# Routed experts in groups of 128 slots with resident down weights, in place of groups of 256 with streamed ones

## The chip, the cores and the metric

The kernel runs on one core of one Trainium2 chip. The metric is the device time of one execution in microseconds (us). A time here is a median over runs; a profile is one further execution, whose own time stands beside its span.

## The reference, cut to what matters

The program is a chain of eight layers over 32 x 128 tokens of 128 features: linear, quantised feed-forward, three attentions, three further feed-forwards. The change lies in the fourth, a mixture of 8 experts in which each token picks 2:

```python
gate_scores = jnp.einsum('bsd,ed->bse', pn, sn) / temperature
top_v, top_i = jax.lax.top_k(gate_scores, 2)
gate_probs = jax.nn.softmax(top_v, axis=-1)
comb = jnp.sum(jax.nn.one_hot(top_i, E, dtype=x.dtype) * gate_probs[..., None], axis=-2)
h = jax.nn.gelu(jnp.einsum('bsd,edf->ebsf', x, W1) + b1[:, None, None, :], approximate=False)
eo = jnp.einsum('ebsf,efd->ebsd', h, W2) + b2[:, None, None, :]
out = jnp.einsum('ebsd,bse->bsd', eo, comb)
```

Here W1 is 128 x 512 and W2 is 512 x 128 per expert, all in f32. The 4096 tokens with 2 choices each make 8192 rows to compute.

## The kernel before, in words

Each layer is one or more blocks; a block ends with all five engines at a barrier. Four blocks make the fourth layer's first part. `route_scores` (L1125) normalises the tokens and makes the scores. `top_two` (L1284) picks two experts per token. `slot_lists` (L1873) sorts the 8192 choices into groups of G x 128 slots, each group of one expert; it writes the token of each slot (`slots`), the expert of each group (`expert_of`) and the slot of each choice (`dest`). Since each expert fills whole groups, the number of groups is fixed at its worst case, NG = (8192 + 8 x (G x 128 - 1)) // (G x 128); with G = 2 that is 39 groups, 9984 slots. All groups are computed, also those that hold only spare rows. The next layer's `combine_project` (L2199) gathers two result rows per token.

`chosen_experts` (L2037) computes the groups. Per group g:

- SP (`load`, L2082) reads the expert number into a register with a value load (L2084), issues the up weights (`wu`, 256 KB, L2088) and the down weights with both biases (`wd`, 322 KB, L2091), then stores the finished group g - 3 (L2095). Buffers are W = 3 deep. SP's queue is in order, so a store or load that waits holds all behind it. Four times it also loads a piece of a mask.
- GpSimd (POOL) gathers the rows of the group with one indirect DMA per 128 slots (L2077).
- PE transposes the rows (`turn`, L2120), then `up` (L2129): four matmuls, 128 features by the group's columns; `down` (L2138): for each 128 slots four accumulating matmuls of 128 columns. Its order is up(g), turn(g+1), down(g-1). One f32 matmul of the program is two weight loads and two passes in the trace.
- ACT applies the Gelu with bias to the four pieces (`gelu`, L2165), and only then copies the transposed rows of the next group out of PSUM (`keep`, L2157).
- DVE adds the output bias (L2195), and does the mask pieces (L2182 to L2185) in between.

`up(g+1)` waits for `keep(g+1)` (L2124), and piece c of it for Gelu c of group g, since both use PSUM bank c (L2128). `down(g)` waits for all four Gelus of g.

Of the kernel before, what the change touches and what calls it, by code (L numbers as in the profile page):

```python
# [13 lines left out]
BF16 = mybir.dt.bfloat16  # L14
# [3 lines left out]
ACT = mybir.ActivationFunctionType  # L18
# [3 lines left out]
P = 128  # L22
D = 128
# [1100 lines left out]
def route_scores(nc, t, d, stage, E, norm):  # L1124


    with ExitStack() as ctx:
# [25 lines left out]
        @block.sync  # L1153
        def _(sp):
            if norm:
                sp.dma_start(vec[:], d[f"{stage}_vec"]).then_inc(loads, 16)
                sp.dma_start(w[:, 0:256], d[f"{stage}_proj"]).then_inc(loads, 16)
                sp.dma_start(temp[:, 0:1], d[f"{stage}_temp"].partition_broadcast(P)).then_inc(loads, 16)
            else:
                sp.dma_start(w[:, 256:256 + E], d[f"{stage}_G"]).then_inc(loads, 16)  # L1160
# [712 lines left out]
def slot_lists(nc, u, stage, E, NG, two_choices):  # L1873
# [14 lines left out]
    with ExitStack() as ctx:  # L1888
# [15 lines left out]

        lo_hot = [sb(f"lo_hot{p}", [P, P, CH], BF16) for p in range(2)]
        lo_table, lo_16 = sb("lo_table", [P, P, CH], BF16), sb("lo_16", [P, NC * CH], BF16)
        hi_hot, hi_num = [sb(f"hi_hot{p}", [P, CH, NHI], BF16) for p in range(2)], [sb(f"hi_num{p}", [P, CH, 2, NHI], BF16) for p in range(2)]
# [129 lines left out]
def chosen_experts(nc, u, d, stage, E, NG, C):  # L2037
# [5 lines left out]
    GS = G * P  # L2043
    W = 3
    n_up = C * P
    width = 2 * C * P + C + D
    MT = 8
    MASK_AT = {3 + 5 * c: c for c in range(NT // MT)}
    with ExitStack() as ctx:
        s = Sems(nc, ctx, stage)  # L2050
        up_came, down_came, x_came, y_stored = ([s.one(f"{n}{p}") for p in range(W)] for n in ("up_came", "down_came", "x_came", "y_stored"))
        x_turned, x_kept, made, acted, down_made, y_ready, load_step, table_in = (
# [6 lines left out]

        wu, wd, xg, y = sbs("wu", [P, n_up], W), sbs("wd", [P, width - n_up], W), sbs("xg", [P, G, D], W), sbs("y", [P, G, D], W)  # L2060
        xgT, h = sbs("xgT", [P, GS], 2), sbs("h", [P, C, GS], 2)
# [18 lines left out]
        @block.sync  # L2080
        def _(sp):
            def load(g):  # L2082
                r = g % W
                e = sp.value_load(u["expert_of"][0:1, g:g + 1], min_val=0, max_val=E - 1)  # L2084
                src = d[f"{stage}_W"][bass.ds(e, 1), :, :].rearrange("e p n -> (e p) n")
                if g >= W:
                    sp.wait_ge(made, C * (g - W + 1))
                sp.dma_start(wu[r][:], src[:, 0:n_up]).then_inc(up_came[r], 16)  # L2088
                if g >= W:
                    sp.wait_ge(y_ready, g - W + 1)  # L2090
                sp.dma_start(wd[r][:], src[:, n_up:width]).then_inc(down_came[r], 16)  # L2091

            def store(g):
                sp.wait_ge(y_ready, g + 1)
                sp.dma_start(u["y_rows"][g * GS:(g + 1) * GS, :].rearrange("(i p) f -> p i f", p=P), y[g % W][:]).then_inc(y_stored[g % W], 16)  # L2095

            def load_mask(c):
                if c >= 2:
                    sp.wait_ge(m_tested[c % 2], c // 2)
                sp.dma_start(u["maski"][c % 2][:], d["mask"][:, c * MT * KEYS:(c + 1) * MT * KEYS]).then_inc(m_came[c % 2], 16)  # L2100

            for g in range(NG):
                load(g)
                if g >= W:
                    store(g - W)
                if g + 1 in MASK_AT:
                    load_mask(MASK_AT[g + 1])
            for g in range(max(NG - W, 0), NG):
                store(g)
            for r in range(W):  # L2110
                sp.wait_ge(y_stored[r], 16 * len(range(r, NG, W)))

        @block.tensor
        def _(pe):
            def turn(g):
                pe.wait_ge(x_came[g % W], 16 * G * (g // W + 1))
                if g >= 2:
                    pe.wait_ge(x_kept, g - 1)
                for i in range(G):
                    ins = pe.transpose(ps[:, 6 + g % 2, i * P:(i + 1) * P], xg[g % W][:, i, :], u["ident"][:])  # L2120
                ins.then_inc(x_turned, 1)

            def up(g):
                pe.wait_ge(x_kept, g + 1)  # L2124
                pe.wait_ge(up_came[g % W], 16 * (g // W + 1))
                for c in range(C):
                    if g >= 1:
                        pe.wait_ge(acted, C * (g - 1) + c + 1)  # L2128
                    pe.matmul(ps[:, c, 0:GS], wu[g % W][:, c * P:(c + 1) * P], xgT[g % 2][:], start=True, stop=True).then_inc(made, 1)  # L2129

            def down(g):
                pe.wait_ge(acted, C * (g + 1))
                pe.wait_ge(down_came[g % W], 16 * (g // W + 1))
                if g >= 2:
                    pe.wait_ge(y_ready, g - 1)
                for i in range(G):
                    for c in range(C):
                        ins = pe.matmul(ps[:, 4 + g % 2, i * P:(i + 1) * P], h[g % 2][:, c, i * P:(i + 1) * P], wd[g % W][:, c * P:(c + 1) * P],  # L2138
                                        start=(c == 0), stop=(c == C - 1))
                ins.then_inc(down_made, 1)  # L2140

            turn(0)
            for g in range(NG):
                up(g)
                if g + 1 < NG:
                    turn(g + 1)
                if g >= 1:
                    down(g - 1)
            down(NG - 1)

        @block.scalar
        def _(sc):
# [5 lines left out]

            def gelu(g, c):
                sc.wait_ge(made, C * g + c + 1)  # L2160
                if c == 0:
                    sc.wait_ge(down_came[g % W], 16 * (g // W + 1))
                    if g >= 2:
                        sc.wait_ge(down_made, g - 1)
                sc.activation(h[g % 2][:, c, :], ps[:, c, 0:GS], ACT.Gelu, bias=wd[g % W][:, C * P + c:C * P + c + 1]).then_inc(acted, 1)  # L2165

            sc.activation(warm[:], u["eps"][:], ACT.Gelu).then_inc(table_in, 1)
            keep(0)
            for g in range(NG):
                for c in range(C):  # L2170
                    gelu(g, c)
                if g + 1 < NG:
                    keep(g + 1)

        @block.vector
        def _(v):
# [11 lines left out]
            for g in range(NG):  # L2188
# [3 lines left out]
                if g >= W:  # L2192
                    v.wait_ge(y_stored[g % W], 16 * (g // W))
                b2 = wd[g % W][:, C * P + C:C * P + C + D]
                v.tensor_tensor(y[g % W][:], ps[:, 4 + g % 2, 0:GS].rearrange("p (i d) -> p i d", d=D),  # L2195
# [540 lines left out]
def build(nc, d, out, stages=range(8)):  # L2736
    with ExitStack() as ctx:
# [67 lines left out]
        def routed(stage, E, NG, G, select, norm, experts, two_choices=False):  # L2805

            with ExitStack() as own:
# [11 lines left out]
                if two_choices:  # L2819
                    u["hots"] = [sb("one", [P, NT, E]), sb("two", [P, NT, E])]  # L2820
                    u["expert_of"] = sb("expert_of", [P, NG], I32)
                else:
                    u["comb"] = sb("comb", [P, E, NT])
# [19 lines left out]
        with ExitStack() as held:  # L2843
            t["maskall"] = held.enter_context(nc.sbuf_tensor("l3x_maskall", [P, NT * KEYS], BF16))
            if 3 in stages:

                PAIR = 2
                NG1 = (2 * NTOK + 8 * (PAIR * P - 1)) // (PAIR * P)
# [71 lines left out]
```

## Time and profile before

| | us |
|---|---|
| median of 3 runs (1444.18 to 1447.78) | 1444.31 |
| the profiled execution | 1442.63 |
| its span | 1440.9 |
| busy PE / DVE / ACT / POOL | 1119.0 / 897.0 / 779.1 / 876.6 |
| first gather to last bias of `chosen_experts` | 426.5 to 583.2 |

The share of busy time is a mean over stages with different limits. To read what this change is worth one looks only at the stretch from 400 to 590 us: which engine is never idle there, how long one group takes from one `up` to the next, and what each other engine waits for.

### The profile page before, as it was taken

To read this page: it belongs to the slowest core of one execution; us is meant where nothing else is said; L and a number is where in the kernel's file an instruction comes from. 1 tells how busy PE (TensorE), PEld (TensorE's weight loads), DVE (VectorE), ACT (ScalarE), POOL (GpSimd) and SP (SyncE) were. 2 spreads that over 40 slices of the span, in tenths; PEclk is the share of its full clock that TensorE was granted. 3 is DMA by queue.
4 is the path that set the end of the run, shared out by engine and by line. 5 is a ranking of instruction groups with operands and counts; after the bars stand their busy time and mean duration, and the time that the engine had idled before them with its cause. 6 is when DMAs were issued, how large, how long until landed. Compare 5 with 4: busy or idle time off the path is not lost. (4 is left out here: it accounts for less than half of the span.)

```text
span 1440.9 us, 26005 instructions
## 1 busy us (share of the span) xinstructions
PE 1119.0 (78%) x9096; PEld 817.8 (57%) x9096; DVE 897.0 (62%) x1829; ACT 779.1 (54%) x1506; POOL 876.6 (61%) x1253
## 2 busy tenths in 40 slices
PE   5682588999429999655688868779997796999993
PEld 5431475666428999455466626646665664566662
DVE  6789867998361211165699958868886387344331
ACT  3478466887434455255588866547776352333220
POOL 5200047998316554476599969648886455588875
PEclk9796698999759999887899979989998596999997
DMA  3000001110037888211111000011110103355542
GB/s 114 8 0 0 0 1 54 44 45 5 4 103 215 244 227 222 64 45 44 54 37 37 20 17 1 0 45 35 34 34 2 77 37 109 80 108 109 109 88 22
DMA packets 62021, 89.96 MB, mean 62 GB/s; under 512 B 10363, under 2 KB 33542, under 8 KB 61638
## 3 DMA queue, kind: packets, MB, share of 16 engines
q1 hardware_dynamic: 46086, 70.07, 15.6%
q0 software_dynamic: 15808, 18.24, 7.8%
q8 instruction: 74, 1.21, 0.3%
q14 instruction: 53, 0.43, 0.1%
HBM read 56.96 MB, written 16.12 MB: 51 GB/s over the span
## 5 line engine op out<-in xcount | busy, mean ns | idle before, releaser
L1692 PE MATMUL ps<-topk_up_sb,topk_wu 128*128 128x512 f32 x256 | 121.6, 611 | 1.2 <-DVE topk_rank_a L1798 1.2
L1492 POOL DMA_INDIRECT out<-topk_shared,l3f_route_slots x64 | 102.4, 1600 | 20.4 <-issue 14.6
L147 POOL TENSOR_SCALAR sb_stage<-sb_x,l0f_rstd,l0f_shift 128x128 f32<-128x128 f32 x48 | 24.5, 526 | 145.7 <-DVE l0f_shift L134 145.5
L1579 ACT ACTIVATE topk_ga<-ps 128x512 f32<-128x512 f32 x64 | 38.5, 602 | 125.0 <-PE ps L1692 125.0
L2165 ACT ACTIVATE l1f_g_h<-ps,l1f_g_wd 128x256 f32<-128x256 f32 x156 | 63.6, 475 | 71.8 <-DMA l1f_g_wd<-l1f_W 39.5
L2195 DVE TENSOR_TENSOR l1f_g_y<-ps,l1f_g_wd 128x256 f32<-128x256 f32 x39 | 16.6, 424 | 135.4 <-PE ps L2138 135.4
L1836 DVE TENSOR_TENSOR sb_xnT<-topk_ga,ps 128x512 f32<-128x512 f32 x64 | 44.0, 687 | 89.9 <-ACT topk_ga L1579 89.8
L2077 POOL DMA_INDIRECT l1f_g_xg<-l1f_rows,l1f_route_slots x78 | 75.1, 963 | 17.7 <-issue 12.5
L2129 PE MATMUL ps<-l1f_g_xgT,l1f_g_wu 128*128 128x256 f32 x312 | 75.4, 385 | 1.6 <-ACT l1f_g_xgT L2157 0.9
L2138 PE MATMUL ps<-l1f_g_wd,l1f_g_h 128*128 128x128 f32 x624 | 75.9, 275 | 0.0
L1488 POOL DMA_INDIRECT topk_xg<-l3f_rows,l3f_route_slots x64 | 63.1, 986 | 19.7 <-issue 17.1
L2138 PEld LDWEIGHTS ps<-l1f_g_wd,l1f_g_h 128*128 128x128 f32 x624 | 72.7, 192 | 0.1
L1692 PEld LDWEIGHTS ps<-topk_up_sb,topk_wu 128*128 128x128 f32 x256 | 46.3, 196 | 44.8 <-issue 42.0
L2251 POOL DMA_INDIRECT l2x_c_yg<-l1f_y_rows,sb_dest x64 | 61.2, 956 | 14.8 <-issue 11.1
L1704 PEld LDWEIGHTS ps<-topk_wd,sb_xnT 128*128 128x128 f32 x512 | 59.0, 192 | 10.0 <-DVE sb_xnT L1836 10.0
L2129 PEld LDWEIGHTS ps<-l1f_g_xgT,l1f_g_wu 128*128 128x128 f32 x312 | 57.2, 193 | 8.9 <-ACT l1f_g_xgT L2157 1.6
L1704 PE MATMUL ps<-topk_wd,sb_xnT 128*128 128x128 f32 x512 | 59.9, 275 | 1.4 <-DVE sb_xnT L1836 1.4
L699 DVE TENSOR_REDUCE l3x_rowmax<-ps 128x16 f32<-128x1232 f32 x32 | 46.0, 1439 | 17.4 <-PE ps L591 17.4
L161 ACT ACTIVATE sb_xnT<-ps 128x512 f32<-128x512 f32 x56 | 33.0, 589 | 38.4 <-PE ps L156 38.3
L662 ACT ACTIVATE l1x_pt<-ps 103x512 f32<-103x512 f32 (+1 forms) x96 | 50.8, 608 | 2.6 <-PE ps L603 2.5
L662 ACT ACTIVATE l3x_pt<-ps 103x512 f32<-103x512 f32 (+1 forms) x96 | 50.5, 608 | 2.6 <-PE ps L603 2.6
L662 ACT ACTIVATE l2x_pt<-ps 103x512 f32<-103x512 f32 (+1 forms) x96 | 50.5, 609 | 1.8 <-PE ps L603 1.7
(530 smaller groups left out, 3510.6 us busy)
## 6 DMA issues: line engine op xcount, KB each, us to landing
l1f_g_wd<-l1f_W SPq DMA_DIRECT2D x39, 322.0 KB, 4.0
l1f_g_wu<-l1f_W SPq DMA_DIRECT2D x39, 256.0 KB, 3.5
topk_wu<-l3f_W SPq DMA_DIRECT2D x16, 512.0 KB, 3.7
l1f_y_rows<-l1f_g_y SPq DMA_DIRECT2D x39, 128.0 KB, 3.9
topk_wd<-l3f_W SPq DMA_DIRECT2D x16, 256.0 KB
l1x_vrows<-sb_l0f_up SPq DMA_DIRECT2D x16, 154.0 KB
l2x_vrows<-l2x_vall SPq DMA_DIRECT2D x16, 154.0 KB
l3x_vrows<-l3x_vall SPq DMA_DIRECT2D x16, 154.0 KB
```

The costliest lines, as they stand in the source:

```text
L662: sc.activation(pt[n % 2][0:rows, c, :, :].rearrange("k g q -> k (g q)"), ps[0:rows, TURN[c], :], ACT.Copy).then_inc(turned_kept, 1)
L699: v.tensor_reduce(rowmax[n % 2][:].rearrange("p (b h) -> p b h", h=HG), scores, X, ALU.max).then_inc(maxed, 1)
L1488: pool.indirect_dma_start(out=xg[g % R][:, i, :], out_offset=None, in_=u["rows"], in_offset=spot(g, i)).then_inc(row_came[g % R], 16)
L1492: pool.indirect_dma_start(out=out_rows, out_offset=spot(g, i), in_=y[g % 2][:, i, :], in_offset=None, compute_op=ALU.add).then_inc(y_added ...
L1692: ins = pe.matmul(ps[:, 2 * (c % 2) + i, :], wu[g % W][:, (i * CX + c) * P:(i * CX + c + 1) * P], xgT[g % 2][:], start=True, stop=True)
L1704: ins = pe.matmul(ps[:, 4 + g % 2, i * P:(i + 1) * P], xh[g % 2][:, c, i * P:(i + 1) * P], wd[g % W][:, c * P:(c + 1) * P], start=(c == 0) ...
L1836: v.tensor_tensor(xh[g % 2][:, c, :], gx[c % 2][:], ps[:, 2 * (c % 2) + 1, :], ALU.mult).then_inc(x_ready, 1)
L2077: pool.indirect_dma_start(out=xg[r][:, i, :], out_offset=None, in_=u["rows"], in_offset=bass.IndirectOffsetOnAxis(ap=u["slots"][:, g * G + ...
L2129: pe.matmul(ps[:, c, 0:GS], wu[g % W][:, c * P:(c + 1) * P], xgT[g % 2][:], start=True, stop=True).then_inc(made, 1)
L2138: ins = pe.matmul(ps[:, 4 + g % 2, i * P:(i + 1) * P], h[g % 2][:, c, i * P:(i + 1) * P], wd[g % W][:, c * P:(c + 1) * P], start=(c == 0), ...
L2165: sc.activation(h[g % 2][:, c, :], ps[:, c, 0:GS], ACT.Gelu, bias=wd[g % W][:, C * P + c:C * P + c + 1]).then_inc(acted, 1)
L2251: pool.indirect_dma_start(out=yg[n % R][:, c, :], out_offset=None, in_=t["y_rows"], in_offset=bass.IndirectOffsetOnAxis(ap=t["dest"][:, c ...
```

## The change

The group is halved (PAIR = 1), which makes 71 groups of 128 slots, 9088 in all. The down weights and both biases of all 8 experts (`held_w`, 5 x 128 + 4 columns each) are loaded once, in `route_scores`, by eight DMAs. PE, ACT and DVE then each read the group's expert number into a register of their own and address `held_w` by it. SP loads the up weights alone. The buffers become 4 deep, the mask pieces come every 10 groups. To make room, three tables of `slot_lists` lie in tiles that exist anyway.

```diff
 def route_scores(...), on SP:
+                for e in range(E):
+                    sp.dma_start(t["held_w"][:, e, :], d[f"{stage}_W"][e, :, 4 * P:]).then_inc(t["w_came"], 16)
 def slot_lists(...):
-        lo_hot = [sb(f"lo_hot{p}", [P, P, CH], BF16) for p in range(2)]
-        lo_table, lo_16 = sb("lo_table", [P, P, CH], BF16), sb("lo_16", [P, NC * CH], BF16)
+        HALF = P * CH // 2
+        by_lo = lambda a: a.bitcast(BF16).rearrange("p (l n) -> p l n", n=CH)
+        lo_hot = [by_lo(u["xc"][:, p * HALF:(p + 1) * HALF]) for p in range(2)]
+        lo_table, lo_16 = by_lo(u["xnT"][:, 0:HALF]), sb("lo_16", [P, NC * CH], BF16)
 def chosen_experts(...):
-    W = 3
+    W = 4
-    MASK_AT = {3 + 5 * c: c for c in range(NT // MT)}
+    MASK_AT = {3 + 10 * c: c for c in range(NT // MT)}
-                src = d[f"{stage}_W"][bass.ds(e, 1), :, :].rearrange("e p n -> (e p) n")
...
-                sp.dma_start(wu[r][:], src[:, 0:n_up]).then_inc(up_came[r], 16)
-                if g >= W:
-                    sp.wait_ge(y_ready, g - W + 1)
-                sp.dma_start(wd[r][:], src[:, n_up:width]).then_inc(down_came[r], 16)
+                sp.dma_start(wu[r][:], d[f"{stage}_W"][bass.ds(e, 1), :, 0:n_up].rearrange("e p n -> (e p) n")).then_inc(up_came[r], 16)
 on PE:
+            def own_weights(g):
+                e = pe.value_load(u["expert_of"][0:1, g:g + 1], min_val=0, max_val=E - 1)
+                return held[:, bass.ds(e, 1), :].rearrange("p e n -> p (e n)")
...
-            def down(g):
+            def down(g, w):
                 pe.wait_ge(acted, C * (g + 1))
-                pe.wait_ge(down_came[g % W], 16 * (g // W + 1))
...
-            down(NG - 1)
+            pe.wait_ge(u["w_came"], 16 * E)
             turn(0)
+            own = own_weights(0)
+            last = None
             for g in range(NG):
                 up(g)
                 if g + 1 < NG:
                     turn(g + 1)
                 if g >= 1:
-                    down(g - 1)
+                    down(g - 1, last)
+                last = own
+                if g + 1 < NG:
+                    own = own_weights(g + 1)
+            down(NG - 1, last)
 on ACT:
-                    sc.wait_ge(down_came[g % W], 16 * (g // W + 1))
...
             for g in range(NG):
+                e = sc.value_load(u["expert_of"][0:1, g:g + 1], min_val=0, max_val=E - 1)
+                biases = held[:, bass.ds(e, 1), C * P:C * P + C].rearrange("p e n -> p (e n)")
                 for c in range(C):
-                    gelu(g, c)
+                    gelu(g, c, biases)
 on DVE:
                 v.wait_ge(down_made, g + 1)
...
-                b2 = wd[g % W][:, C * P + C:C * P + C + D]
+                e = v.value_load(u["expert_of"][0:1, g:g + 1], min_val=0, max_val=E - 1)
+                b2 = held[:, bass.ds(e, 1), C * P + C:width - n_up].rearrange("p e n -> p (e n)")
 def build(...):
+                    u["held_w"] = sb("held_w", [P, E, 5 * P + 4])
+                    u["w_came"] = own.enter_context(nc.semaphore(stage + "_w_came"))
...
-                PAIR = 2
+                PAIR = 1
```

On ACT, one group in a row of the program before, from one copy of transposed rows (`xgT`) to the next:

```order
L2157 ACTIVATE l1f_g_xgT<-ps 128x256
L2165 ACTIVATE l1f_g_h<-ps,l1f_g_wd 128x256 x4
L2157 ACTIVATE l1f_g_xgT<-ps 128x256
```

and one group now; TENSOR_LOAD with ISA x2 is the value load, and each single ISA is a register operation that makes an address:

```order
L2167 ACTIVATE l1f_g_xgT<-ps 128x128
L2178 TENSOR_LOAD l1f_route_expert_of
L2178 ISA x2
L2173 ISA
L2173 ACTIVATE l1f_g_h<-ps,l1f_route_held_w 128x128
L2173 ISA
L2173 ACTIVATE l1f_g_h<-ps,l1f_route_held_w 128x128
L2173 ISA
L2173 ACTIVATE l1f_g_h<-ps,l1f_route_held_w 128x128
L2173 ISA
L2173 ACTIVATE l1f_g_h<-ps,l1f_route_held_w 128x128
L2167 ACTIVATE l1f_g_xgT<-ps 128x128
```

The value load stands between the copy for a group and its first Gelu, and the wait for each matmul is on the ISA ahead of each Gelu.

On PE, one group of the program before, from `up` to `up` (`wu` and `wd` are the streamed weights, `h` the Gelu's output):

```order
L2129 MATMUL ps<-l1f_g_xgT,l1f_g_wu 128x256 x4
L2120 MATMUL ps<-sb_ident,l1f_g_xg 128x128 x2
L2138 MATMUL ps<-l1f_g_wd,l1f_g_h 128x128 x8
L2129 MATMUL ps<-l1f_g_xgT,l1f_g_wu 128x256 x4
```

and one group now:

```order
L2134 MATMUL ps<-l1f_g_xgT,l1f_g_wu 128x128 x4
L2121 MATMUL ps<-sb_ident,l1f_g_xg 128x128
L2142 ISA
L2142 MATMUL ps<-l1f_route_held_w,l1f_g_h 128x128
L2142 ISA
L2142 MATMUL ps<-l1f_route_held_w,l1f_g_h 128x128
L2142 ISA
L2142 MATMUL ps<-l1f_route_held_w,l1f_g_h 128x128
L2142 ISA
L2142 MATMUL ps<-l1f_route_held_w,l1f_g_h 128x128
L2125 TENSOR_LOAD l1f_route_expert_of
L2125 ISA x2
```

The value load for the next group stands between `down` and the next `up`, in the queue of the engine that is never idle before.

## Rows read from the trace of the kernel before

**Rows 1.** Stretch (from:to, length): busy us (instructions) by engine, clock, DMA share, GB/s.

```profile
445.00:570.00 125.00, 124.39 (x865) 115.63 (x865) 20.29 (x45) 62.16 (x165) 68.93 (x98) 1.00 0.85 236
```

**Rows 2.** Timeline of PE (start, us, what), two groups late in the stage.

```profile
569.81 1.89 PE L2129 MATMUL ps<-l1f_g_xgT,l1f_g_wu 128*128 128x256 f32 x8
571.54 0.38 PE L2120 MATMUL ps<-sb_ident,l1f_g_xg 128*128 128x128 f32 x2
571.76 1.95 PE L2138 MATMUL ps<-l1f_g_wd,l1f_g_h 128*128 128x128 f32 x16
573.54 1.89 PE L2129 MATMUL ps<-l1f_g_xgT,l1f_g_wu 128*128 128x256 f32 x8
```

**Rows 3.** Groups by line, 433 to 584: count, busy us, mean ns, idle before.

```profile
L2138 PE MATMUL ps<-l1f_g_wd,l1f_g_h 128*128 128x128 f32 x624 | 75.9, 275 | 0.0
L2129 PE MATMUL ps<-l1f_g_xgT,l1f_g_wu 128*128 128x256 f32 x312 | 75.4, 385 | 1.6 <-ACT l1f_g_xgT L2157 0.9 <-issue 0.6
L2165 ACT ACTIVATE l1f_g_h<-ps,l1f_g_wd 128x256 f32<-128x256 f32 x156 | 63.6, 475 | 71.8 <-DMA l1f_g_wd<-l1f_W 39.5 <-PE ps L2129 32.3
L2195 DVE TENSOR_TENSOR l1f_g_y<-ps,l1f_g_wd 128x256 f32<-128x256 f32 x39 | 16.6, 424 | 135.4 <-PE ps L2138 135.4
L2184 DVE TENSOR_REDUCE sb_row_any<-l1f_g_nonzero 128x8 f32<-128x616 f32 x4 | 3.2, 794 | 0.1
```

**Rows 4.** Timeline of ACT, same two groups.

```profile
570.93 1.57 ACT L2165 ACTIVATE l1f_g_h<-ps,l1f_g_wd 128x256 f32<-128x256 f32 x4 [1.81 <-DMA l1f_g_wd<-l1f_W]
574.18 1.77 ACT L2165 ACTIVATE l1f_g_h<-ps,l1f_g_wd 128x256 f32<-128x256 f32 x4 [1.40 <-PE ps L2129]
```

**Rows 5.** Timeline of ACT in the attention before, an operation 128 columns wide.

```profile
322.82 0.36 ACT L681 ACTIVATE l1x_gated<-ps,sb_gate 128x128 f32<-128x128 f32 x1
323.07 1.57 ACT L662 ACTIVATE l1x_pt<-ps 103x512 f32<-103x512 f32 x3
```

**Rows 6.** Groups by line and shape on ACT: one without a per-partition operand.

```profile
L1198 ACT ACTIVATE ps<-ps 128x128 f32<-128x128 f32 x32 | 8.5, 266 | 3.6 <-PE ps L1182 3.6
```

**Rows 7.** SP's lines 2084 (to 500 us) and 2088: ns min/median/max, first and last start.

```profile
L2084 SPq TENSOR_LOAD <-l1f_route_expert_of x19: 263/273/827, 425.6 to 496.8; - x19
L2084 SPq FUSED_REGOPS  x19: 152/152/192, 426.1 to 497.6; - x19
...
L2088 SPq FUSED_REGOPS  x39: 42/42/48, 426.4 to 572.0; - x39
...
DMA to landing us min/median/max: 2.7/3.5/4.4
```

**Rows 8.** Timeline of SP, 473 to 478.

```profile
473.38 0.43 SPq L2095 DMA_DIRECT2D l1f_y_rows<-l1f_g_y  x1
474.57 0.34 SPq L2088 DMA_DIRECT2D l1f_g_wu<-l1f_W  x1
```

**Rows 9.** Timeline, all engines: end of `slot_lists`, start and end of `chosen_experts`.

```profile
422.62 0.48 DVE L2025 TENSOR_REDUCE l1f_slots_eid<-l1f_slots_begun 128x39 f32<-128x312 f32 x1
...
423.66 0.24 DVE L2029 SCALAR_TENSOR_TENSOR l1f_slots_slot<-l1f_slots_nums 128x78 f32<-128x78 f32 x1 [0.34 <-ACT l1f_slots_nums L1954]
...
427.99 0.96 POOL L2077 DMA_INDIRECT l1f_g_xg<-l1f_rows,l1f_route_slots  x1 [0.30 <-issue]
...
432.48 0.69 PE L2120 MATMUL ps<-sb_ident,l1f_g_xg 128*128 128x128 f32 x2 [9.27 <-DMA l1f_g_xg<-l1f_rows,l1f_route_slots]
...
433.64 3.20 PE L2129 MATMUL ps<-l1f_g_xgT,l1f_g_wu 128*128 128x256 f32 x8 [0.47 <-ACT l1f_g_xgT L2157]
...
437.50 0.38 ACT L2157 ACTIVATE l1f_g_xgT<-ps 128x256 f32<-128x256 f32 x1
...
437.93 1.99 PE L2129 MATMUL ps<-l1f_g_xgT,l1f_g_wu 128*128 128x256 f32 x8 [0.47 <-ACT l1f_g_xgT L2157]
...
582.78 0.42 DVE L2195 TENSOR_TENSOR l1f_g_y<-ps,l1f_g_wd 128x256 f32<-128x256 f32 x1 [1.36 <-PE ps L2138]
...
586.13 0.35 SPq L2238 DMA_DIRECT2D sb_wstat<-l2x_W  x1
```

More of the change, by code:

```diff
@@ L2047, in chosen_experts @@
     MT = 8
-    MASK_AT = {3 + 5 * c: c for c in range(NT // MT)}
+    MASK_AT = {3 + 10 * c: c for c in range(NT // MT)}
     with ExitStack() as ctx:
         s = Sems(nc, ctx, stage)
-        up_came, down_came, x_came, y_stored = ([s.one(f"{n}{p}") for p in range(W)] for n in ("up_came", "down_came", "x_came", "y_stored"))
+        up_came, x_came, y_stored = ([s.one(f"{n}{p}") for p in range(W)] for n in ("up_came", "x_came", "y_stored"))
         x_turned, x_kept, made, acted, down_made, y_ready, load_step, table_in = (
@@ L2058, in sbs @@
             return [ctx.enter_context(nc.sbuf_tensor(f"{stage}_g_{name}{p}", shape, F32)) for p in range(n)]
-        wu, wd, xg, y = sbs("wu", [P, n_up], W), sbs("wd", [P, width - n_up], W), sbs("xg", [P, G, D], W), sbs("y", [P, G, D], W)
+        wu, xg, y = sbs("wu", [P, n_up], W), sbs("xg", [P, G, D], W), sbs("y", [P, G, D], W)
+        held = u["held_w"]
         xgT, h = sbs("xgT", [P, GS], 2), sbs("h", [P, C, GS], 2)
@@ L2137, in down @@
                     for c in range(C):
-                        ins = pe.matmul(ps[:, 4 + g % 2, i * P:(i + 1) * P], h[g % 2][:, c, i * P:(i + 1) * P], wd[g % W][:, c * P:(c + 1) * P],
+                        ins = pe.matmul(ps[:, 4 + g % 2, i * P:(i + 1) * P], h[g % 2][:, c, i * P:(i + 1) * P], w[:, c * P:(c + 1) * P],
                                         start=(c == 0), stop=(c == C - 1))
                 ins.then_inc(down_made, 1)
+            pe.wait_ge(u["w_came"], 16 * E)
             turn(0)
+            own = own_weights(0)
+            last = None
             for g in range(NG):
@@ L2157, in keep, with gelu @@
                 sc.activation(xgT[g % 2][:], ps[:, 6 + g % 2, 0:GS], ACT.Copy).then_inc(x_kept, 1)
-            def gelu(g, c):
+            def gelu(g, c, biases):
                 sc.wait_ge(made, C * g + c + 1)
-                if c == 0:
-                    sc.wait_ge(down_came[g % W], 16 * (g // W + 1))
-                    if g >= 2:
-                        sc.wait_ge(down_made, g - 1)
-                sc.activation(h[g % 2][:, c, :], ps[:, c, 0:GS], ACT.Gelu, bias=wd[g % W][:, C * P + c:C * P + c + 1]).then_inc(acted, 1)
+                if c == 0 and g >= 2:
+                    sc.wait_ge(down_made, g - 1)
+                sc.activation(h[g % 2][:, c, :], ps[:, c, 0:GS], ACT.Gelu, bias=biases[:, c:c + 1]).then_inc(acted, 1)
             sc.activation(warm[:], u["eps"][:], ACT.Gelu).then_inc(table_in, 1)
```

## The prediction

> **What bounds the kernel now.** I read the page's slices first, then the table of stretches, then the timeline and the groups by line of 400 to 590 us. In the stage that the change rewrites PE is busy 124.4 of 125 us at a granted clock of 1.00, which is its upper level of 2.4 GHz [rows 1]; ACT is busy 62, POOL 69, DVE 20, and the DMA rings carry 236 GB/s at a share of 0.85. PE's timeline shows the beat: one `up` starts at 569.81, the next at 573.54, so a group of 256 slots takes 3.73 us [rows 2], and 39 of them 145.6. The idle columns of the other engines [rows 3] are waits in PE's shade: ACT sits idle 39.5 us for `wd`, yet PE's own idle ahead of `up` and `down` is 1.6 and 0.0. So the `wd` traffic that the change removes is worth nothing by itself. What can be won is PE's work on padding; what can be lost is the slack that lets everything else hide.
>
> **PE's work per group.** Eight passes of `up` at 256 columns start 0.216 us apart ((1.89 - 0.379)/7, the last one's end taken from its duration of about 0.38); sixteen passes of `down` at 128 columns 0.112 us apart ((1.95 - 0.275)/15); a transpose takes (571.76 - 571.54)/2 = 0.11 [rows 2, 3]. At 128 slots: 8 x 0.112 + 0.105 + 8 x 0.112 = 1.90, and 1.91 with the 0.01 by which the present 3.73 exceeds its own parts. 71 x 1.91 = 135.6 against 145.6: 10 us less if PE stays the bound. Both `up` and `down` then run at 128 columns, a width whose cost the `down` row already shows.
>
> **The beat is halved, so latencies come into sight.** `up(g+1)` needs the transposed rows, which ACT copies only after the four Gelus of group g. That chain, from one `up` to the next:
> - `up` starts to the first Gelu: 573.54 to 574.18, 0.64 [rows 2, 4], of which two passes are 0.216 + 0.379 = 0.60 and 0.045 is the passing on. At 128 columns: 0.112 + 0.275 + 0.045 = 0.43.
> - The new register operation that carries the wait ahead of each Gelu: one takes 0.042 us on SP, the heavier one of the value load 0.152 [rows 7], and from the starts (426.1, 426.4) some 0.05 lies between such steps. I take 0.14; bounds 0.04 and 0.2. The next three hide behind the Gelu that runs.
> - Four Gelus: when nothing holds them, 256-wide ones start (1.57 - 0.475)/3 = 0.365 apart [rows 3, 4]; a 128-wide one with a per-partition operand lets the next start after 0.25 (322.82 to 323.07) [rows 5]. I take 0.26 and bounds 0.25 and 0.365: 1.04 us.
> - The copy of 128 columns: 0.266 for a like operation [rows 6], 0.38 at 256 [rows 9]. I take 0.29. Then 0.05 until `up` starts (437.88 to 437.93) [rows 9].
>
> Sum 0.43 + 0.14 + 1.04 + 0.29 + 0.05 = 1.95 us, a hair above PE's 1.91. Before, the same chain was 0.64 + 4 x 0.365 + 0.38 + 0.05 = 2.5 of 3.73. So the bound moves to this loop, and the beat T is 1.95.
>
> **The value loads.** The trace shows one only on SP: 0.273 + 0.152 and the gaps between its steps, about 0.56 us in all [rows 7]. None of PE, ACT, DVE has ever run one here. Queued behind it are: on ACT the first Gelu's wait, on PE the next `up`, on DVE the bias sum. On ACT it stands behind the copy; if the queue goes on while the engine works, it begins when the last Gelu starts, 1.35 after `up`, and is done at 1.9, before the next group's first matmul at 1.95 + 0.4: free. On PE it begins once `down` has been handed over, about 0.6 us after `up` starts, done at 1.2, and `up` needs it at 1.95: free. On DVE it lies after the wait, so the bias sum ends later: 2.06 (last pass of `down` after 0.9 + 0.1 + 0.78 + 0.275) + 0.04 + 0.56 + 0.14 + 0.29 = 3.09 us after the `up` in front of it; nobody but the store needs it. The bounds of this term are 0 and, on PE, the whole 0.56 with the array's run-out on top (a rival below).
>
> The row gives 0.56 us for a value load. The Trainium skill, page "Advanced Engine Details and Errata", Sequencer Loop, says that control instructions run in the sequencer's microcode while other engine instructions can be read and queued; by that rule the loads hide, as taken here. But the Trainium skill's page "DMA: Bandwidth & Descriptors", Latency and other measured facts, puts a `tensor_load` at some 600 ns and says that the compiler unrolls to spread it; the SP row agrees, and an unhidden one per group would by that page be 71 x 0.6 = 43 us. No run here shows yet which of the two holds on PE.
>
> **The up weights.** SP's order is load(g+1) after store(g-4). Store of a group starts 3.14 after the `up` that follows the group's own; from a store to the next `wu` issue are 474.57 - 473.38 = 1.19, value load included [rows 8]; landing takes 2.7 to 4.4, median 3.5 [rows 7]. So 4T >= 3.14 + 1.19 + landing + 0.05. The median of now gives T >= 1.97; but now the ring also carries `wd`: a group's traffic falls from 834 KB per 3.73 us to 384 KB per 1.95 (224 to 197 GB/s), and a store of half the size is all that is just ahead. I take a landing of 3.2, T >= 1.90: not the bound, though close. Where a mask piece on DVE (0.79 and two lighter operations [rows 3]) delays a bias sum, by up to 0.8 as I estimate, the slack is gone; four times 0.4 = 1.6 us. The new `held_w` loads (8 x 322 KB) go out in `route_scores`, behind the small ones, and have some 35 us. POOL needs a gather (0.96 + 0.30) and a small operation per group [rows 9], under 1.6: hidden.
>
> **Before, at the start and at the end.** In `slot_lists` tables shrink by 9% (78 to 71), while four operations over 312 elements at 0.48 us grow to 568 elements; 0.34 us of idle stands behind them [rows 9]. Gain and loss are each under 1 us; I take 0. At the start the first transposes waited for the second gather (issued 427.99, used 432.48); with one gather per group the last needed one is issued 1.3 earlier. The first `up` ran at the low clock, 3.20 instead of 1.89 [rows 9, 2]; I leave 1.5 us for that. From the last `up`: its four Gelus end at 1.65, `down` starts at 1.8, ends 2.86, and the bias sum 3.85 with the value load; from there to the next block 586.13 - 583.20 = 2.93 [rows 9].
>
> **Sum.** The next block starts at (433.64 - 1.3) + 1.5 + 70T + 3.85 + 2.93 + 1.6 = 442.2 + 70T. With T = 1.95 that is 578.7 against 586.13: 7.4 us less. The profiled execution, 1442.63, would become 1435.2; it lies 1.7 below the median of the runs, 1444.31, from which the same difference gives **1436.9**. The same time as before comes at T = 2.06. What a measurement of this kernel can tell from no change is about 0.3%, 4.3 us: T below 1.995 is faster, above 2.12 slower.
>
> **Rivals.**
> - *The up weights come late.* The landing stays at 3.5 to 3.9 because gathers and stores are now more and smaller: T = (4.38 + 3.5)/4 = 1.97 up to 2.07, 1438 to 1445. For it: the rings were 85% busy, and the formula has no slack. Against: less traffic. Its place is PE's idle ahead of `up`, released by DMA.
> - *ACT can't hide its value load.* It starts only when the copy is done: per group 1.04 + 0.29 + 0.56 + 0.14 + 0.05 = 2.08, 1446; if the register operations also widen the Gelus' spacing to 0.30, 2.24, 1457. It decides from a spacing or load that adds 0.11 to T. For it: no engine with a datapath has run such a load here.
> - *PE can't hide its own.* The load waits for the array to run out: 1.91 + 0.16 + 0.56 = 2.63 per group, 442.2 + 184.1 = 626.3, 40 us more, 1484. Against: semaphore waits and many weight loads on PE already pass ahead of the array, whose idle is 0.0 [rows 3].
> - *PE stays the bound throughout* (T = 1.91, no mask loss): 4.4 better than the forecast, 1432.5. Same side, inside the range.
>
> **Chances.** The forecast with the last case, T under 2.0: 0.54. Late weights: 0.18, mostly within 0.3%. ACT's load: 0.16, a third of it within 0.3%. PE's load: 0.12. So faster 0.55, within 0.3% 0.20, slower 0.25. The range reaches from 1431 (PE bound, start gain whole) to 1452 (T = 2.16, half of the ACT case), and leaves out a little under 2 in 10, all of it above. The forecast's own range is 1432 to 1440.
>
> **What would show it.** Right: `up` to `up` near 1.95; PE's idle about 0.04 per group, ended by ACT's copy; the passes of `down` 0.112 apart despite their register addresses; Gelus 0.26 apart; value loads on PE with the array busy beside them; the next block's first load near 579. Wrong: gaps of half a microsecond ahead of every `up` with nothing released (PE's load), a Gelu that starts more than 0.5 after its matmul's end (ACT's), or idle ahead of `up` released by `wu` (late weights). A granted clock below 1.00 in the steady part would upset all of it, since every pass is counted at the upper level.

## The result: slower by 0.4%, and the profile after

The changed kernel takes 1449.89 us (median of 15 runs, 1446.97 to 1456.75) against 1444.31 for the kernel before, measured beside it: a ratio of 1.0038, 95% interval 1.0027 to 1.005. The forecast was 1436.9, faster; the time lies inside its range of 1431 to 1452, the sign is wrong. The profiled execution took 1447.0 us with a span of 1445.3, 4.4 more than the one of before.

The stretch of [rows 1], in the same columns: PE is busy 117.9 of 125 us where it was 124.4, the granted clock is still 1.00, its upper level, and the rings carry 195 GB/s in place of 236.

```profile
445.00:570.00 125.00, 117.94 (x991) 114.58 (x989) 23.59 (x70) 76.44 (x292) 67.43 (x117) 1.00 0.73 195
```

Two undisturbed groups, PE, ACT and SP in the timeline (start, us, what), the counterpart of [rows 2, 4, 8]. Below, a step is the time from one `up` to the next, the beat is the median step, the landing of a load is the time from its issue to the last of its signals, and its lead is the time from its issue to the `up` that uses it:

```profile
451.34 1.16 PE L2134 MATMUL ps<-l1f_g_xgT,l1f_g_wu 128*128 128x128 f32 x8
451.67 0.34 SPq L2092 DMA_DIRECT2D l1f_g_wu<-l1f_W  x1
451.97 1.14 ACT L2173 ACTIVATE l1f_g_h<-ps,l1f_route_held_w 128x128 f32<-128x128 f32 x4 [0.69 <-PE ps L2134]
...
452.44 1.06 PE L2142 MATMUL ps<-l1f_route_held_w,l1f_g_h 128*128 x8
...
452.99 0.29 ACT L2167 ACTIVATE l1f_g_xgT<-ps 128x128 f32<-128x128 f32 x1
...
453.33 0.97 PEld L2134 LDWEIGHTS ps<-l1f_g_xgT,l1f_g_wu 128*128 128x128 f32 x8
453.33 1.16 PE L2134 MATMUL ps<-l1f_g_xgT,l1f_g_wu 128*128 128x128 f32 x8
```

The beat is 453.33 - 451.34 = 1.99 (the median over the stage is 1.998), and the chain is the one forecast: `up`, 0.63 to the first Gelu, 1.02 to the copy (four Gelus), 0.29 of copy, 0.05 to the next `up`. And then this, in the very next group:

```profile
454.59 0.91 SPq L2096 DMA_DIRECT2D l1f_y_rows<-l1f_g_y  x1
...
454.98 0.29 ACT L2167 ACTIVATE l1f_g_xgT<-ps 128x128 f32<-128x128 f32 x1
...
456.96 0.52 PEld L2134 LDWEIGHTS ps<-l1f_g_xgT,l1f_g_wu 128*128 128x128 f32 x4 [1.66 <-issue]
457.00 0.57 PE L2134 MATMUL ps<-l1f_g_xgT,l1f_g_wu 128*128 128x128 f32 x3 [1.50 <-issue]
```

The copy is done at 455.27, yet `up` of group 10 starts at 457.00 and not at 455.33. Its weights were issued at 451.67, 5.3 us before that. PE's wait ahead of this `up` can only be for `up_came`; the profile calls it "issue", since it names no releaser. The trace's semaphore records settle it: a load gives sixteen signals, and of this one's fifteen came by 3.26 us after the issue and the last at 5.23, which is 456.90, 0.06 ahead of PE's first weight load. Over the stage (the line's own answer: us, times; a stop counts twice, once for PE's matmuls and once for its weight loads):

```profile
L2134 PE MATMUL ps<-l1f_g_xgT,l1f_g_wu x568: 274/275/579, 432.3 to 585.6; 128*128 128x128 f32 x190
its engine sat idle before it (us, times) until:
  issue: 13.3, 14
  ACT l1f_g_xgT L2167: 6.8, 13
```

In before these were 1.5 and 2.5 us. Counting the `up`s in the timeline, the steps that exceed the beat by over 0.1 are 13 from group 6 on, 9.7 us in all, the largest before groups 10, 15, 21, 27, 33, 39, 49, 56, 62 and 68. These ten make 9.1 us and are late weights. The other three (42, 51, 60, together 0.6 us) are not: they come at the same groups when the up weights are loaded four times only (below), where a Gelu of ACT starts some 0.2 late. Start and end of the stage, the counterpart of [rows 9]:

```profile
432.28 2.05 PE L2134 MATMUL ps<-l1f_g_xgT,l1f_g_wu 128*128 128x128 f32 x8 [0.54 <-ACT l1f_g_xgT L2167]
...
435.05 2.08 PE L2134 MATMUL ps<-l1f_g_xgT,l1f_g_wu 128*128 128x128 f32 x8 [0.51 <-ACT l1f_g_xgT L2167]
...
438.84 1.76 PE L2134 MATMUL ps<-l1f_g_xgT,l1f_g_wu 128*128 128x128 f32 x8
```

```profile
588.59 0.29 DVE L2206 TENSOR_TENSOR l1f_g_y<-ps,l1f_route_held_w 128x128 f32<-128x128 f32 x1 [0.69 <-issue]
591.58 0.34 SPq L2249 DMA_DIRECT2D sb_wstat<-l2x_W  x1
```

The next block starts at 591.58, 5.45 later than before and 12.9 later than forecast. The last `up` starts at 584.74, so the tail is 6.84 where 3.85 + 2.93 was forecast; its parts are 4.14 to the end of the bias sum and 2.70 behind it, so two errors cancel there.

### The profile page after: what moved, and what is told of

Read it like the earlier page. It is cut to its first block and busy times, and to the rows that moved or that the text cites. A ratio compares the mean times of both kernels' runs of the same rounds, so it can differ in the third digit from the quotient of the medians.

```text
span 1445.3 us, 28221 instructions
## 1 busy us (share of the span) xinstructions
PE 1118.4 (77%) x9289; PEld 823.4 (57%) x9289; DVE 901.4 (62%) x1861; ACT 796.9 (55%) x1666; POOL 875.2 (61%) x1278
## 5 line engine op out<-in xcount | busy, mean ns | idle before, releaser
L2173 ACT ACTIVATE l1f_g_h<-ps,l1f_route_held_w 128x128 f32<-128x128 f32 x284 | 82.2, 368 | 60.6 <-PE ps L2134 59.9
L2206 DVE TENSOR_TENSOR l1f_g_y<-ps,l1f_route_held_w 128x128 f32<-128x128 f32 x71 | 20.6, 290 | 135.5 <-PE ps L2142 106.4
L2134 PE MATMUL ps<-l1f_g_xgT,l1f_g_wu 128*128 128x128 f32 x568 | 84.2, 293 | 8.7 <-issue 7.5
L2134 PEld LDWEIGHTS ps<-l1f_g_xgT,l1f_g_wu 128*128 128x128 f32 x568 | 71.2, 197 | 13.1 <-ACT l1f_g_xgT L2167 5.8
L2142 PE MATMUL ps<-l1f_route_held_w,l1f_g_h 128*128 x568 | 75.8, 277 | 0.0
L1490 POOL DMA_INDIRECT topk_xg<-l3f_rows,l3f_route_slots x64 | 62.8, 981 | 19.7 <-issue 17.7
L2082 POOL DMA_INDIRECT l1f_g_xg<-l1f_rows,l1f_route_slots x71 | 68.3, 963 | 10.3 <-issue 0.8
L2142 PEld LDWEIGHTS ps<-l1f_route_held_w,l1f_g_h 128*128 128x128 f32 x568 | 69.9, 194 | 0.1
L1049 PE MATMUL ps<-sb_xnT,sb_l0f_wT 128*128 128x512 f32 x96 | 44.8, 620 | 8.8 <-ACT sb_l0f_up L968 7.0
```

The costliest lines, as they stand in the source:

```text
L1049: ins = pe.matmul(ps[:, 3 * (j % 2) + c, :], wT[:, (first + c) * P:(first + c + 1) * P], t["xnT"][:, j * BLK:(j + 1) * BLK], start=True, s ...
L1490: pool.indirect_dma_start(out=xg[g % R][:, i, :], out_offset=None, in_=u["rows"], in_offset=spot(g, i)).then_inc(row_came[g % R], 16)
L2082: pool.indirect_dma_start(out=xg[r][:, i, :], out_offset=None, in_=u["rows"], in_offset=bass.IndirectOffsetOnAxis(ap=u["slots"][:, g * G + ...
```

## The experiments

All but the last two ran on three other chips, on which the kernel before takes 1483 to 1484 us; on the one where it was profiled its routed stage ends at the same time as before (586.35), so stage times compare. The table gives, from each profile, first `up` to last `up`, the beat, the idle ahead of `up` called "issue" (us, times, each stop counted on PE's matmuls and on its weight loads, so about double), the steps that exceed the beat by over 0.1 from group 6 on (us, times), and the start of the next block.

| kernel | ratio to before, 95% | up to up | beat | "issue" | long steps | next block |
|---|---|---|---|---|---|---|
| before, rerun | 1.0013 (0.9991 to 1.0034) | 144.9 | 3.735 | 3.5, 9 | 1.8, 6 | 586.35 |
| changed, rerun | 1.0021 (1.0000 to 1.0041) | 154.3 | 2.002 | 20.3, 25 | 12.5, 18 | 593.40 |
| later store | 0.9962 (0.9945 to 0.9978) | 143.9 | 1.998 | 2.6, 7 | 1.2, 5 | 582.75 |
| up weights loaded once | 0.9947 (0.9927 to 0.9967) | 144.4 | 2.002 | 0.7, 3 | 0.9, 4 | 584.21 |
| copy early | 0.9999 (0.9978 to 1.0021) | 152.6 | 1.968 | 24.2, 24 | 14.1, 14 | 592.82 |
| later store, copy early | 0.9899 (0.9880 to 0.9918) | 135.1 | 1.896 | 1.9, 4 | 0.5, 3 | 574.50 |
| DVE's load first | 0.9963 (0.9942 to 0.9984) | 145.6 | 1.998 | 4.3, 6 | 2.7, 5 | 584.49 |
| pairs, weights held | 0.9996 (0.9981 to 1.0011) | 143.7 | 3.734 | 1.7, 2 | none | 586.69 |
| small groups, streamed | 1.0092 (1.0064 to 1.0120) | 165.6 | 2.21 | 41.6, 63 | most | 605.73 |
| later store, copy early, warm passes | 0.9924 (0.9901 to 0.9947) | 134.9 | 1.896 | 1.2, 3 | 0.6, 3 | 573.91 |
| later store, copy early, DVE's load first | 0.9881 (0.9859 to 0.9902) | 135.5 | 1.896 | 1.1, 2 | 0.2, 2 | 572.94 |
| later store, value loads twice | 1.0072 (1.0048 to 1.0096) | 158.2 | 2.207 | 8.3, 29 | 1.0, 7 | 598.13 |

**The store one group later.**

```diff
                 load(g)
-                if g >= W:
-                    store(g - W)
+                if g >= W + 1:
+                    store(g - W - 1)
```

> The changed kernel, but SP issues the store of group g-5 behind the load of group g, not that of g-4. Theory (late up weights: SP's queue waits for the bias sum of g-4 before it can read the next expert number and issue the next load, which leaves 3.65 us until use, while some landings take 4 to 5.3): the lead grows to about 5.5 us, the 13 stalls of 0.2 to 2.0 us ahead of up go, every beat is 2.00 and the kernel takes 9 us less than the changed one: about 1440, ratio to before 0.997. Rival (the rings themselves are late, through instruction fetches and small packets, by whatever lead): less than half of it comes back, 1446 or more. Rival (the stalls come from something on PE or ACT): no change, 1449.

The long steps fell from 12.5 to 1.2 us and the median lead rose to 5.6. The work of a group is the same, instruction fetches come as often, and six loads still land after 4.0 to 4.9 us, but none of them stops PE now: the stalls came from late landings together with the short lead. The next block starts 10.7 us earlier than in the rerun; the gain in the timed ratio is 0.006, or 9 us, as expected. In 445 to 570 PE is busy again:

```profile
445.00:570.00 125.00, 124.61 (x1056) 122.11 (x1055) 24.92 (x74) 81.39 (x310) 71.38 (x123) 1.00 0.77 205
```

**No loads of up weights after the fourth group** (most groups then use a wrong W1).

```diff
-                load(g)
+                if g < W:
+                    load(g)
```

> The changed kernel, but the up weights are loaded only for the first four groups and then used again, so most groups compute with another expert's W1. Theory: no load can be late; beat 2.00 throughout, ended by ACT's copy, about 1440 as in the kernel whose store is later. Rival (gathers, not weights, are late): stalls remain, now put down to the gathered rows. Rival (the beat of 2.00 is itself lengthened by the traffic beside it): the beat falls to the forecast 1.95 or below, 1436.

The same 144 us, at 75 GB/s in place of 205:

```profile
445.00:570.00 125.00, 124.77 (x1056) 122.14 (x1055) 24.94 (x74) 81.68 (x310) 72.17 (x124) 1.00 0.27 75
```

So the beat of 2.00 owes nothing to this traffic, and the later store had already recovered what late weights cost.

**ACT's copy before the fourth Gelu, with the later store.**

```diff
                 for c in range(C):
+                    if c == C - 1 and g + 1 < NG:
+                        keep(g + 1)
                     gelu(g, c, biases)
-                if g + 1 < NG:
-                    keep(g + 1)
```

> As the kernel with the later store, and ACT copies the next group's transposed rows before the fourth Gelu instead of after it. Theory (the steady beat is the chain up, Gelus, copy, up on ACT): the next up no longer waits for the last Gelu, PE becomes the bound at 1.91 to 1.93 a group, 71 x 0.08 = 6 us less than with the later store alone: about 1434, ratio 0.993. Rival (PE's value load or register operations set 2.00): the beat stays 2.00, 1440.

The beat is 1.896, which is seventeen passes 0.112 apart: PE is bound by its own passes.

```profile
478.27 1.06 PE L2134 MATMUL ps<-l1f_g_xgT,l1f_g_wu 128*128 128x128 f32 x8
479.16 0.27 PE L2121 MATMUL ps<-sb_ident,l1f_g_xg 128*128 128x128 f32 x1
479.27 0.94 PE L2142 MATMUL ps<-l1f_route_held_w,l1f_g_h 128*128 x7
```

Eight passes of `up` now take 1.06. In the changed kernel they take 1.16 each time PE had to wait for the copy: the pass behind the first one starts after 0.21 us and not after 0.11 as the others do.

**The early copy alone.**

> The changed kernel with ACT's copy of the next rows before the fourth Gelu, the store left where it is. Theory (two loops stand side by side: ACT's at 2.00 and the up weights' at (4.38 + landing)/4, landing being about 3.4 us until usable, 1.95): the gain of the early copy (1.90 instead of 2.00, 7 us) is mostly eaten, since the lead falls by 4 x 0.1: beats of 1.95 with waits ahead of up in most groups, stalls of the same groups longer: 2 to 4 us less than the changed kernel, ratio 1.001 to 1.0025. Rival (stalls come from isolated late landings only and the loop of the weights is not near): all 7 us come, ratio 0.999.

Undisturbed groups do run at 1.90, but the four-group lead shrinks with the beat, and PE waits more for weights: against 1.896 the steps from group 6 on are 17.7 us too long. From first to last `up` it takes 152.6, between the two traces of the changed kernel (152.5, 154.3), although ACT's loop is 7 us shorter: in the trace the time came back as waits. The timed ratio, 0.9999, does not decide: its interval holds the rival's 0.999 and overlaps the changed kernel's, 1.0000 to 1.0041.

```profile
DVE l1f_g_y L2206 <- issue: 84.2, 46, 3.2
POOL l1f_g_for_load L2080 <- PE ps L2121: 46.0, 57, 2.2
ACT l1f_g_h L2173 <- PE ps L2134: 36.9, 41, 2.8
DVE l1f_g_y L2206 <- PE ps L2142: 14.6, 8, 2.9
PEld ps L2134 <- issue: 12.2, 12, 2.2
PE ps L2134 <- issue: 10.2, 10, 2.1
```

(Waits in 445 to 570: us in total, times, longest. The last two lines are the same stops, counted twice.)

**DVE's value load ahead of its wait for `down`.**

```diff
+                e = v.value_load(u["expert_of"][0:1, g:g + 1], min_val=0, max_val=E - 1)
                 v.wait_ge(down_made, g + 1)
...
-                e = v.value_load(u["expert_of"][0:1, g:g + 1], min_val=0, max_val=E - 1)
```

> The changed kernel with DVE's value load ahead of its wait for down instead of behind it, so that the bias sum, the store and the next load of up weights come 0.56 us earlier. Theory (late up weights by their short lead): each of the 13 stalls shrinks by up to 0.5, some 6 of the 9.7 us of them go; ratio 0.9995 to 1.001. Rival (SP's store alone, or fetches, set the stalls): no change, 1.0038.

More came than expected: long steps fell from 12.5 us (rerun) to 2.7, and the ratio is 0.9963 where 0.9995 to 1.001 was expected. Half a microsecond on the engine that nobody but the store waits for was most of the loss.

**Each part alone.** Pairs with held weights (`PAIR = 2`, `W = 3`, mask pieces every 5), and the kernel before with `PAIR = 1`, `W = 4`, mask pieces every 10:

> One part of the change alone: groups of 256 as before (39, three buffers, mask pieces every 5), with the down weights and biases resident and read by a register per group. Theory (PE is the bound, value loads and register operations pass beside its work): beat 3.73 as before, 1444, ratio 0.999 to 1.002; ring traffic falls from 224 to about 138 GB/s and the small idle ahead of up goes (1 to 2 us less at most). Rival (the value load on PE costs some of its time each group): 39 x 0.3 to 0.56 = 12 to 22 us more.

> The other part of the change alone: 71 groups of 128 slots, four buffers, mask pieces every 10, but the down weights and biases streamed for every group as before, no value loads on PE, ACT or DVE. Traffic is 71 x 0.71 MB = 50 MB instead of 39 x 0.83 = 33 MB. Theory (the rings carry at most about 236 to 244 GB/s here): 0.71 MB / 0.24 = 2.95 us a group, 71 x 2.95 = 210 us instead of 146, some 60 us slower than before, 1505 to 1510, ratio 1.04 to 1.05. Rival (PE or ACT's loop binds and residency was not needed): near 2.0 a group, 1448.

Holding the weights is worth nothing where PE is bound, as forecast. Small groups with streamed weights are slower, but far less than I expected: a step takes 165.6/70 = 2.37 us on average, not 2.95, because the rings carried 313 GB/s at a share of 0.97. The 236 GB/s of before was demand, not a ceiling; I had read it as one.

```profile
445.00:570.00 125.00, 108.36 (x892) 102.17 (x890) 21.68 (x65) 68.56 (x263) 60.88 (x106) 1.00 0.97 313
```

**Warm passes.**

```diff
             pe.wait_ge(u["w_came"], 16 * E)
+            for _ in range(14):
+                pe.transpose(ps[:, 5, 0:P], u["ident"][:], u["ident"][:])
             turn(0)
```

> The kernel with the later store and the early copy, and 14 transposes of the identity into an unused bank on PE while it waits for the first gathered rows. Theory (the first three groups run at the low clock because PE was idle 8.2 us before them: beats 2.63, 2.72, 1.89 instead of 1.90): up to 1.5 us less, the granted clock of 432 to 438 at 1.00 instead of 0.5, ratio 0.989. Rival (the clock does not rise in that time, or the warm passes delay the first transposes): 0 to 2 us more than without.

```profile
432.23 1.13 PE L2134 MATMUL ps<-l1f_g_xgT,l1f_g_wu 128*128 128x128 f32 x8 [0.64 <-ACT l1f_g_xgT L2169]
433.20 0.27 PE L2121 MATMUL ps<-sb_ident,l1f_g_xg 128*128 128x128 f32 x1
433.95 2.07 PE L2134 MATMUL ps<-l1f_g_xgT,l1f_g_wu 128*128 128x128 f32 x8 [0.47 <-ACT l1f_g_h L2175]
```

The first `up` ran at passes of the upper level (1.13), the second was slow again (2.07): the granted clock is 0.85 in 432.2 to 433.9 and 0.50 in 433.9 to 436.0. The ratio can't be told from that without the warm passes (0.9899): no gain that can be measured, and neither theory nor rival as written.

**Value loads twice on PE and on ACT**, with the later store:

```diff
+                pe.value_load(u["expert_of"][0:1, g:g + 1], min_val=0, max_val=E - 1)
                 e = pe.value_load(u["expert_of"][0:1, g:g + 1], min_val=0, max_val=E - 1)
```

and the same on ACT.

> The kernel with the later store, with each value load on PE and on ACT made twice. In its trace one load takes 0.30 + 0.15 and its gaps, about 0.56 us, and has 0.4 us of slack behind it on PE and 0.6 on ACT. Theory (they hide beside matmuls and Gelus): ACT's second one is still hidden, PE's comes out by at most 0.1 to 0.2 a group: 7 to 14 us more at most, ratio 1.001 to 1.006. Rival (a value load stops its engine's datapath or costs its full time): 0.56 a group, 40 us more.

```profile
471.11 1.13 PE L2135 MATMUL ps<-l1f_g_xgT,l1f_g_wu 128*128 128x128 f32 x8
472.07 0.27 PE L2121 MATMUL ps<-sb_ident,l1f_g_xg 128*128 128x128 f32 x1
472.18 1.06 PE L2143 MATMUL ps<-l1f_route_held_w,l1f_g_h 128*128 x8
473.29 1.13 PE L2135 MATMUL ps<-l1f_g_xgT,l1f_g_wu 128*128 128x128 f32 x8
```

These groups take 2.18 instead of 2.00 (the median is 2.21), with passes 0.11 apart as before: 0.18 to 0.21 of a second load's 0.65 shows (0.30 + 0.15 and gaps). It is PE's: there the second load ends at 473.12 and `up` starts at 473.26, while ACT's ends at about 473.6, before its next Gelu. The first load was hidden, and the slack behind it was about 0.45. The timed ratio is 0.011 above the later store's, 16 us; I had allowed 14. The two ran on different chips, but the stage is 15 us longer too.

**All three edits** (later store, early copy, DVE's load first).

> The three edits together: later store, copy before the fourth Gelu, DVE's value load ahead of its wait. Theory (PE alone binds at 1.90 once the up weights have a longer lead): the beat stays 1.90 and the two or three small stalls of up to 0.3 that are left come from something else, so it equals the kernel with the first two edits, ratio 0.988 to 0.992. Rival (the left stalls are still late weights): 0.5 us less.

It beats the kernel before by 1.2% and the changed one, run on the same chip, by 1.3%; its interval overlaps that of the first two edits. No wait for late weights is left in its steady part.

**The kernels themselves again.**

> The kernel before itself, as a run of its own on the chip of these comparisons, for its profile and as a measure of the comparison. Expected: ratio 0.998 to 1.002; the next block's first work at 589.1 and few waits ahead of up, as in the trace of before, if its routed stage runs here as it did there; if up weights are late more often on this chip, before's stage ends 3 to 6 us later too, which would explain why the comparisons so far came out 3 to 6 us better than the stage's end in each trace.

> The changed kernel itself, beside the experiments on their chip. Expected from its first measurement: ratio 1.003 to 1.005, some 13 stalls ahead of up in its trace, next block's first work at 594.5. If before loses more on this chip than the changed kernel does, the ratio is below 1.002.

On this chip the changed kernel is slower by 0.2%, and the interval reaches down to no change; by the end of the stage it is 7.1 us behind. Before's stage ends no later than it did, so my explanation for comparisons that look 3 to 6 us better than the stage's end is not borne out. The intervals are 3 us each way, but most of these comparisons lean to the same side; the cause stays open.

**What makes one load in seven late.** Redundant waits on PE, ahead of the groups, make its instruction stream longer; the second kernel has 64 of them, all at the first place. Each ran once (1449.28 and 1444.48, before 1447.12), so only their traces count.

```diff
+                for _ in range(84):
+                    pe.wait_ge(u["w_came"], 16 * E)
             product(0)
...
-            pe.wait_ge(u["w_came"], 16 * E)
+            for _ in range(45):
+                pe.wait_ge(u["w_came"], 16 * E)
             turn(0)
```

> The changed kernel with 128 further waits on PE, all for a semaphore that has long fired, placed where PE idles ahead of the groups (84 in slot_lists, 44 at the start of chosen_experts), so that PE's instruction stream is 128 instructions longer there. In the changed kernel the up weights come late at groups 10, 15, 21, 27, 33, 39, 50, 56, 62, 68, and 16 KB instruction fetches run within 2 us of just those loads (453.4, 464.4, 476.9, 489.7, 503.0, 516.3, 539.3, 551.9, 565.3, 577.4). PE takes 44 instructions a group, so a fetch of some 256 every 6 groups would be its own. Theory (a load beside such a fetch lands late): fetches and late groups both move 128/44 = 2.9 groups earlier: about 12, 18, 24, 30, 36. Rival (mask pieces, gathers or the loop's own phase make a group late): they stay at 15, 21, 27, 33, 39.

> The same with 64 further waits, all in slot_lists. Theory: the fetches and late groups move by 1.5 groups: about 13 or 14, 19 or 20, 25 or 26, 31 or 32, 37 or 38. Rival: they stay at 15, 21, 27, 33, 39.

In the trace PE has only 64 and 32 instructions more, so the shifts to expect are 1.5 and 0.7 groups. Groups with a step over 2.3, first the changed kernel, then with 64 more, then with 32 more:

```text
10 15 21 27 33 39 49 56 62 68
 8 13 20    32 37 43 49 55 61 66
   13 21    32 33 38 44    56    67
```

In the changed kernel a 16 KB instruction fetch of PE runs while each of these ten loads is in flight. With 64 more, eight moved by 1 or 2 groups, one (49) stayed, one (27) vanished and one (43) is new, and again all ten stand at a fetch. With 32 more, six of eight stand at a fetch; the loads of the other two (13, 33) landed after 3.4 and 3.2 but had been issued late. It is no strict rule: the fetch at 530.6 in the changed kernel made no load late, and in its rerun group 29 was late without one. The DMA queues of two stretches, the changed kernel's 502 to 505 and the shifted one's 499.5 to 502.5:

```profile
DMA packets 481, 0.77 MB, mean 256 GB/s; under 512 B 68, under 2 KB 198, under 8 KB 480
q8 instruction: 1, 0.02, 2.5%
```

```profile
DMA packets 410, 0.60 MB, mean 198 GB/s; under 512 B 52, under 2 KB 194, under 8 KB 409
q8 instruction: 1, 0.02, 2.0%
```

and the `up`s behind them, group 33 of the changed kernel and 32 of the shifted:

```profile
506.80 1.13 PE L2134 MATMUL ps<-l1f_g_xgT,l1f_g_wu 128*128 128x128 f32 x8 [1.87 <-issue]
```

```profile
503.76 1.13 PE L2137 MATMUL ps<-l1f_g_xgT,l1f_g_wu 128*128 128x128 f32 x8 [1.23 <-issue]
```

The late groups follow PE's instruction stream, not the group number: mask pieces and gathers stayed where they were. PE did not starve for instructions itself, since with the later store the fetches come as often and the stalls are gone. The semaphore records show what is late: in the load of group 10 fifteen of sixteen signals came by 3.26 us and the last at 5.23, in that of group 62 by 3.57 and at 4.81, in group 43 of the first shifted kernel by 3.34 and at 4.68. So one part in sixteen is late, by up to 2 us, and the fetch's own packet takes 0.9 to 1.9 us on its engine. That the late part is the one whose DMA engine carried the fetch fits this, but the trace does not name a packet's engine: it is argued, not shown.

## Why the prediction was wrong, point by point

The last `up` was forecast at 432.3 + 1.5 + 1.6 + 70 x 1.95 = 571.9 and came at 584.7. Of the 12.8, 3.4 are the beat, 1.6 the start, 7.5 late weights beyond the 1.6 allowed and 0.6 the three other long steps; that is 13.1, and many steps that are a little shorter than the median take 0.3 back. Without the late weights the sign would have been right: the later store and the weights loaded once are both faster than before.

- **The step that failed: the up weights.** I took a landing of 3.2, found T >= 1.90 and wrote "not the bound, though close". The form was right: 4T less the lead of 3.66 is 4.33, where I had 3.14 + 1.19 + 0.05. By the semaphore records of the trace the median landing is 3.43 and `up` starts 0.09 after it, so the lead is just enough. But I compared a typical landing with the lead where [rows 7] gave a spread of 2.7 to 4.4, and then chose below the median because of less traffic. That spread was itself too narrow: the profile could tell the landing of 13 of the 39 loads, and the semaphore records of all 39 reach 5.5. A landing over 3.6 stops PE unless an earlier stop has just lengthened the lead, and the loss is not caught up, since ACT's loop has no slack either. The cost is the sum over the slow landings, 9.1 us, against the 1.6 that I gave the mask pieces. The rival "late weights" had the mechanism, but as a uniform T up to 2.07 it had the wrong shape and was too small: the next block's 591.58 is 442.2 + 70T at T = 2.13.
- **The lead itself** was cut by DVE's value load behind its wait, which "nobody but the store needs". Its 0.56 was in my 3.14, but I did not see what it was worth: the store stands ahead of the next load in SP's queue. Moving two lines took 9.8 of the rerun's 12.5 us of long steps away.
- **The beat**: 1.998, not 1.95. Gelus, copy and passing on came close to the forecast (1.02 for 1.04, 0.29, 0.05). The register operation was 0.11 rather than 0.14; `up` to the end of its second pass was 0.10 longer, the slower second pass after a wait. 70 x 0.048 = 3.4 us. The register-addressed `down` passes are 0.11 apart, as forecast.
- **The start**: the first `up` at 432.28 (forecast 432.3; the other traces of groups of 128 with held weights have 431.4 to 433.5, so the match is partly luck). Steps of 2.77, 3.79 and 2.60, with a granted clock of 0.50, 0.50 and 0.71, cost 3.1 and not 1.5.
- **Value loads** hide on PE and ACT, as forecast; both rivals on them fall (one load free, of a second 0.18 to 0.21). By the Trainium skill, "Advanced Engine Details and Errata", Sequencer Loop, other engine instructions can be read and queued while a control instruction executes in the sequencer's microcode; the trace agrees, with loads of 0.30 on PE and 0.28 on ACT beside busy datapaths. The figure of some 600 ns for a `tensor_load` in the Trainium skill's "DMA: Bandwidth & Descriptors", Latency and other measured facts, fits one whole load with its register step here, 0.54 to 0.65, as latency and not as cost.
- **The tail**, 6.84 against 6.78, is right by luck: 0.29 more to the end of the bias sum, 0.23 less behind it. **Residency worth nothing by itself** (0.9996): right.
- **PE alone at 1.91**: right, 1.896, once both loops around it were loosened. The 10 us that smaller groups promised are there: 144.9 to 135.5 from `up` to `up`, and the next block 13.4 earlier.

## What to carry to other kernels

When a beat is halved, write down each resource's lead in beats and in us, and compare it with the slowest landings of the trace, not with the median: one late load in seven cost 9 us here, more than the change won. Look in an in-order queue for what stands ahead of a prefetch, and follow that back through every engine, also those "nobody waits for". And loosen all loops that lie within a few per cent of each other together: the early copy alone gave nothing that the trace shows, with the later store it gave 9 us.

## What was not expected of the hardware

- The stream of instructions shows in the data's time: with some 44 PE instructions a group, a 16 KB fetch came about every 12 us, and beside nine of the eleven from 453 us on a load landed 0.5 to 1.8 us later than the median of 3.43.
- The DMA rings carried 313 GB/s at a share of 0.97 where 236 at 0.85 had been seen.
- The first f32 pass of `up` after a wait for ACT's copy is followed after 0.21 us, after one for weights after 0.18, and not after 0.11.
- After 14 warm passes the granted clock was up for one `up` (1.13 us) and down again (0.50) in the next, with PE idle 0.64 us ahead of the first and 0.47 ahead of the second.
